# Last stage of an audio-tower kernel: the product's 1168 columns divided into 512, 512 and 144 in place of 390, 390 and 388

## What is computed

```python
h = h + ffn(layernorm(h))

def ffn(x):
    base_out = einsum('btd,od->bto', x, base_W) + base_b           # 1024 -> 1024
    logits   = einsum('btd,nd->btn', x, router_W) + router_b       # 1024 -> 15
    probs    = softmax(logits); topk_p, topk_i = top_k(probs, 8)
    w        = weight of each of the 8 experts, from topk_p and expert_map
    a        = einsum('btd,erd->bter', x, A)                       # 1024 -> 8 x 16
    lora     = einsum('bter,eor->bto', a * w[..., None], B) * 2.0  # 128 -> 1024
    return base_out + lora
```

## Time and profile before

| | |
|---|---|
| median of 3 runs | 2593.61 us (2593.51 to 2594.55) |
| the profiled execution's own time | 2587.67 us |
| its span, first to last instruction | 2586.0 us |
| PE busy | 2431.7 us (94%), 15004 matmuls |
| PEld (weight loads) busy | 2111.5 us (82%), 15004 loads |
| DVE busy | 1635.5 us (63%) |
| ACT / POOL busy | 1187.8 (46%) / 1000.5 (39%) |
| mean granted TensorE clock | 0.974 |
| last stage, PE from the first transpose to the last matmul | 2188.27 to 2581.49 us |

### The profile page before, as it was taken

The page is one execution under the profiler, slowest core; times in us unless marked ns, Lnnn a source line. Parts: engine busy times, 40 slices in busy tenths (PEclk is TensorE's granted clock), DMA queues, the critical chain, the costliest instruction groups (busy, mean ns, idle before and its releaser), DMA issues. The chain is left out here.

```text
span 2586.0 us, 45893 instructions
## 1 busy us (share of the span) xinstructions
PE 2431.7 (94%) x15004; PEld 2111.5 (82%) x15004; DVE 1635.5 (63%) x3318; ACT 1187.8 (46%) x3624; POOL 1000.5 (39%) x852
## 2 busy tenths in 40 slices
PE   8999999986899988999999999799999997999998
PEld 6888878865566658999999999688888885899998
DVE  8875587894366657888888898511111113777775
ACT  5664444441345548999999999511111111111110
POOL 5764676772023226667666767100000001011110
PEclk9999999998899999999999999899999998999999
DMA  7654587676466541111111111533333333212211
GB/s 249 201 173 142 184 257 244 209 229 226 136 197 201 194 149 67 46 44 47 40 47 43 47 45 39 198 113 98 97 97 97 97 97 102 69 66 73 75 65 49
DMA packets 202314, 313.61 MB, mean 121 GB/s; under 512 B 20784, under 2 KB 157488, under 8 KB 202032
## 3 DMA queue, kind: packets, MB, share of 16 engines
q1 hardware_dynamic: 194256, 282.54, 34.2%
q0 software_dynamic: 7184, 25.69, 2.5%
q10 hardware_dynamic: 720, 3.67, 0.4%
HBM read 230.05 MB, written 81.79 MB: 121 GB/s over the span
## 5 line engine op out<-in xcount | busy, mean ns | idle before, releaser
L1871 POOL TENSOR_TENSOR ffn_res<-shared_h,ffn_bias 128x1024 f32<-128x1024 f32 x24 | 60.3, 2516 | 852.4 <-DMA ffn_bias<-base_b 555.9
L1512 ACT ACTIVATE attn_prob<-attn_prob,attn_bias 94x94 f32<-94x94 f32 x1024 | 366.9, 361 | 43.4 <-DVE attn_bias L1589 42.0
L740 PE MATMUL up_ps<-up_t_lo,up_s_hi 128*128 128x502 f32 (+1 forms) x840 | 333.5, 397 | 23.2 <-DVE up_t_lo L655 23.1
L741 PE MATMUL up_ps<-up_t_hi,up_s_lo 128*128 128x502 f32 (+1 forms) x840 | 329.8, 393 | 0.0
L742 PE MATMUL up_ps<-up_t_hi,up_s_hi 128*128 128x502 f32 (+1 forms) x840 | 329.0, 392 | 0.0
L1721 DVE TENSOR_TENSOR out_x_lo<-out_raw,out_x_hi 128x512 fp32r<-128x512 f32 x96 | 66.5, 692 | 399.3 <-ACT out_x_hi L1706 399.3
L506 POOL TENSOR_TENSOR up_both<-up_raw 128x502 f32<-128x502 f32 (+1 forms) x150 | 240.3, 1606 | 118.3 <-DVE up_t_lo L655 84.9
L1706 ACT ACTIVATE out_x_hi<-out_raw 128x512 fp32r<-128x512 f32 x96 | 60.6, 632 | 434.7 <-PE out_ps_h L243 284.5
L1628 POOL TENSOR_TENSOR attn_prob<-attn_prob,attn_share 94x752 f32<-94x752 f32 x128 | 184.6, 1442 | 179.5 <-DVE attn_share L1597 179.5
L243 PE MATMUL out_ps_h<-out_w_hi,out_x_lo 128*128 128x512 f32 x768 | 238.1, 391 | 11.2 <-DVE out_w_lo L228 11.2
L243 PE MATMUL out_ps_h<-out_w_lo,out_x_hi 128*128 128x512 f32 x768 | 237.3, 390 | 0.0
(11 more groups left out here) (227 smaller groups left out, 5760.5 us busy)
## 6 DMA issues: line engine op xcount, KB each, us to landing
up_raw<-x_f SPq DMA_DIRECT2D x240, 251.0 KB, 3.4
up_w_raw<-w SPq DMA_DIRECT2D x120, 256.0 KB, 4.1
up_raw<-x_f SPq DMA_DIRECT2D x120, 250.0 KB, 3.7
out_raw<-o_t SPq DMA_DIRECT2D x96, 256.0 KB, 4.3
o_t<-attn_o_t SPq DMA_DIRECT2D x128, 188.0 KB, 1.9
shared_ring<-wo SPq DMA_DIRECT2D x32, 512.0 KB, 6.6
y<-down_y POOLq DMA_DIRECT2D x24, 512.0 KB, 3.4
out_y<-y SPq DMA_DIRECT2D x24, 512.0 KB, 5.7
```

What stands on the lines that cost most here:

```text
L740: nc.tensor.matmul(o, sh, tl, start=(kk == 0), stop=False)
L741: nc.tensor.matmul(o, sl, th, start=False, stop=False)
L1512: last = nc.scalar.activation(prob[u % NPR][0:SEQ, h, part], prob[u % NPR][0:SEQ, h, part], ACT.Exp, bias=bias[u % 2][0:SEQ, n:n + 1], sca ...
```

## The change

The cuts move from 0, 390, 780, 1168 to 0, 512, 1024, 1168. The base columns then fill two banks exactly, and the third bank holds only experts and router (A_AT = 0, R_AT = 128). The base product still has three matmuls for each pass and block, now 512, 512 and 144 wide. The lora product and DVE's addition have two pieces of 512 in place of three of 390, 390 and 244.

```diff
 ER = EXP * RANK
 FW = DM + ER + NR + 1
-CUT = [0, 390, 780, FW]
+CUT = [0, DM // 2, DM, FW]
 A_AT = DM - CUT[2]
 R_AT = A_AT + ER
@@ DVE, the sum that leaves the stage
-                    for c in range(3):
-                        a, e = CUT[c], min(CUT[c + 1], DM)
+                    for c in range(2):
+                        a, e = CUT[c], CUT[c + 1]
                         last = nc.vector.tensor_tensor(o[u % 2][:, a:e], ps_o[u % 2][c][:, 0:e - a],
                                                        res[u % 3][:, a:e], ALU.add)
                     last.then_inc(o_done, 1)
@@ PE, the lora product
-                    ends = [(CUT[c], min(CUT[c + 1], DM)) for c in range(3)]
+                    ends = [(CUT[c], CUT[c + 1]) for c in range(2)]
                     last = three_pass(nc, [ps_o[u % 2][c][:, 0:e - a] for c, (a, e) in enumerate(ends)], ht_hi[:],
                                       ht_lo[:], [b_hi[:, 0, a:e] for a, e in ends], [b_lo[:, 0, a:e] for a, e in ends],
                                       False, True, onto=True)
```

## The result

The changed kernel took 2609.88 us (median of 6 runs, 2604.15 to 2611.64), the kernel before 2593.56 in the same comparison (6 runs, 2584.97 to 2594.55). The ratio is 1.0067, with a 95% interval of 1.0056 to 1.0078: slower by 14 to 20 us. The profiled execution took 2610.57 us, with a span of 2608.9.

The account below looks back on a forecast made before the run. TensorE's matmuls, one behind the other, were taken to bound the last stage. Base product +17.4, lora -1.0 and DVE's addition -0.1 made +16.3 us on the median 2593.61: 2609.9 us, range 2604.5 to 2618.

Parts of the forecast that it names:

- Base product: Last stage, PE: each base pass goes from 536 to 567 ns, +31 ns; +17.4 us in sum.
- I keep these 3: 229 ns: 512-wide base matmul in the last stage: 226 ns as in attn_out, plus the 3 ns base pays over lora.
- Transposes as the load: Last stage, PE: 128-wide transposes start every 0.109 us, taken as the weight load and the 144-wide matmul's cost.
- Lora: Last stage, PE: two 512-wide matmuls a pass, 453 ns in place of 467; 69 passes count, -1.0 us.
- Start of the stage: Tile 0's 0.7 us vanish in PE's 3.89 us wait for xn; half clock in tile 1 adds 0.4 us.
- PE waits for nobody: Last stage: PE never waits, while DVE has 2.5 us to spare in a step of 15.27.
- Everything else at nothing: Logits, hw, ACT, POOL, SP and weight splitting cost nothing more; no wait is added.
- DVE's two additions: End of the run: two 512-wide operations take 1.28 us in place of three at 1.35; -0.1 us in the last tile.
- one mark: Timeline sign in the last stage: the matmul behind the 144-wide one starts 0.109 us after it, whatever its pass.
- rival 1: Last stage: load does not bind behind the 144-wide matmul; pass 531 ns, -3.8 us, 2589.8 us; chance 0.05.
- Rival 2: Last stage: group starts at 512 and 1024 also save the 3 ns; pass 525 ns, -7 us, 2586.5; chance 0.03.
- Rival 3: Last stage: 512-wide matmuls at tok_down's 233 ns, narrow one at 129; +59 ns a pass, 2626 us; chance 0.09.

Follow-up runs that it names:

- the last run: Kernel before with cuts 384 and 768, weight rows and stationary tiles re-placed, tok_up's moving tiles 512 elements apart, tok_down's g_hi, g_lo moved 224 bytes: 2569.88 us, ratio 0.9914.

## Why the prediction was right, point by point

The forecast was 2609.9 us, +16.3; measured were 2609.88, +16.3. The mechanism holds: TensorE is the bound, a matmul can't be shorter than the weight load behind it, and the 144-wide one pays 108 ns for 60 ns of columns. The run with 16 columns and the one without the matmul show it from both sides. That the sum agrees to the last digit is luck: the later steps grew by more than I said, and the start of the stage and two short waits gave back more.

- *Base product.* I took +31 ns a pass, 0.74 us in the 24 passes of a step. The step shows 0.81, or 34 ns a pass. (The 39 ns read above hold for 22 of the 24; in the other two the narrow matmul stands before a transpose and costs 66 ns.) The 109 of the load were right. The failing step is "I keep these 3: 229 ns" for a 512-wide matmul: it was 232 to 234. I had `attn_out`'s 226 and `tok_down`'s 233 and laid this stage near the first. Of these stages only `attn_out` has 226, and 32 bytes undo it. What I built on, that a lora matmul pays 13 ns and a base one 16, was a mean over unlike widths. By the starts in the earlier trace rows the 390-wide lora matmuls take (2432.88 - 2432.52) / 2 = 0.18 us, 17 ns over their columns, and the 244-wide one some 0.11, at most 9 over. So the 3 ns that I kept were no cost of the base product.
- *Transposes as the load.* That 109 ns is the load is borne out by the one-column and the 16-column matmuls. The transposes, from which I took it, don't show it (see above): right number, in part for a wrong reason.
- *Lora.* I took -14 ns a pass, -1.0 us in all, by 226 ns for each matmul. By the loads it is 0.464 us in place of 0.467, so -0.2 us in all. The same step failed.
- *Start of the stage.* I let tile 0 vanish in PE's wait of 3.89 us, and tile 1 had 0.4 us for half the clock and some 0.6 for its other passes. In the profiled execution after, the wait was 0.36, and tile 1 did not see the half clock; `xn` came earlier against PE. From the first transposes of the stage to the third (2226.39 - 2196.36 against 2219.78 - 2188.27) it took 30.0 us in place of 31.5, tile 1's step 16.17 in place of 16.88: 2.2 us less where I had +1.0. It need not be the change's: the kernel before with 32 bytes of padding took 30.1 us as well. But the six profiled executions with the changed kernel's cuts and all its matmuls took 30.0 to 30.2 us, and those with other cuts 30.0 to 30.2 in three and 31.4 to 31.7 in four, so whether the change has a part in it is open. A price of one execution for a race between a DMA and PE should have stood in the range only.
- *Waits that went away.* I wrote that PE waits for nobody. That fails for two of the 18 steps, which the same view of waits has (kernel before, 2290 to 2560 us):

```profile
PEld ffn_ps_o L243 <- DVE ffn_ht_lo L1986: 0.8, 2, 0.4
```

  These two steps took 15.66 and 15.57 us. In the changed kernel PE comes later to the lora product, no step of tiles 2 to 22 has this wait, and 0.7 us are won that I had at nothing.
- *Everything else at nothing* held. DVE's two additions took 1.29 us at the end in place of 1.35, and no new wait came up.

So the last stage gave 22 x 0.81 = 17.8 us in the steps of tiles 2 to 23, less 0.7 for the waits, and -2.2 at its start: +14.9 in the profiled pair, 408.1 us in place of 393.2. The spans differ by 22.9, not 14.9: the other 8 us are in stages the change does not touch, `tok_down` above all (327 against 320 us, with four more stretches at half the clock). That is why the median, and not the pair of spans, is to be compared with the sum; and the +16.3 of the medians hold such differences too.

I had named one mark wrongly: the matmul behind the 144-wide one would start 0.109 us after it. It is recorded 0.066 after it, and the loads are 0.108 apart. Read by that row alone, rival 1 (the load does not bind, 73 ns) would look true; the loads' own starts, and the 276 ns of the next slot, refute it. The Trainium skill ("TensorE: Matmul & The Clock Gate", section "LDWEIGHTS (loading the stationary operand)") gives a load as its columns divided by 1.2, which makes 107 ns for 128 columns of weights (an estimate from the page's formula); the loads here are 0.108 apart around a narrow base matmul, and the runs agree. The section "Back-to-back issue gap" of that page gives some 131 ns as the sustained spacing of 512-wide matmuls in a real stream; no stream of 512-wide matmuls in the stages read here has less than 226, and the measurement decides.

Rival 2 (faster) has nothing for it. Rival 3 was half right: `tok_down`'s 233 ns came, the 129 of L1190 did not (L1190's own loads are 109 to 112 ns apart). Its reason, other engines at work beside PE, is not needed: in `attn_out` 32 bytes alone did as much. For the last stage it isn't excluded, since there 512-wide matmuls stayed dear with their operands placed as in `attn_out`.

## What to carry to other kernels

Where each matmul has a weight load of its own, divide columns so that none is narrower than a load (here about 240 columns at 2.4 GHz); equal groups are safe, and filling banks to 512 with a small rest is not. Below that width price the matmul by the load behind it, not by its columns, and read spacing from PEld's starts. Before you take one kind of instruction as a measure of the load, check that its own time can't be what you see. Where memory allows, try rows, stationary tiles and starts of column groups of a float32r product at one place modulo 512 bytes: with the other edits of the last run it brought 0.9% here, but it did not help every product, so measure each stage.

## What the runs showed of the hardware that I had not expected

- A pad of 32 bytes ahead of the stationary tiles raised the cost of each 512-wide matmul in `attn_out` from 226 to 234 ns; 64 bytes did the same. With both operands at one place modulo 512 bytes the surplus over the columns is 13 ns in `attn_out` (512 wide) and in the last stage's base product with cuts at 384 and 768 (384 and 400 wide). But it is 16 ns in `tok_down` (229), 15 and 18 in `tok_up` (502 and 500 wide), and stays at 18 to 21 in the last stage with cuts at 512 and 1024. The 384-wide matmuls of `tok_down` pay 13 to 14 whether their tiles are 224 bytes off that place or at it. Where the places differ, wide matmuls else pay 15 to 22. So place counts, the rule is not complete, and why is open. Whether the narrow matmul itself keeps the 512-wide ones at 232 wasn't tried apart from that.
- The 144-wide matmul costs 108 ns with a base matmul behind it and some 66 with a transpose behind it: the floor belongs to the load that follows.
- Plain float32 matmuls 384 wide start every 322 ns, float32r ones of the same width every 173 or 174 (both in `tok_down`, kernel before).
- A matmul behind a narrow one is recorded as started before its weights can be in (66 ns behind a 144-wide one, 27 behind a 16-wide one), and the next slot is longer by as much as is missing to 108.
- With the step at 14.7 us a round through DVE and PE begins to bind: as long as it stands, there is no more than 0.5 us a step to be had in this stage from TensorE alone.
